# A fused attention, feed-forward and read/write layer on one core: the table of unit-matrix matmuls is emptied

## The reference

```python
x = x + layer(_layernorm(x), pos, ctx)     # read, attention, write, read, MLP, write
x = x + ffn(_layernorm(x))

def rat_read(res, W, gamma, beta, n):      # H = 256 channels of C = 4 copies
    y = einsum('blhc,hoc->bloh', res.reshape(b, l, H, C), W)
    return layernorm over h of y, times gamma plus beta

# attention: 16 heads of 16, rope, causal softmax over 512 rows, per batch
# rat_write: y @ wod.T, y @ wab.T + b, softplus and exp gates, hs * A + out * B

def _binary_diff_weight(w, base):          # for w1, w2, w3 (3584 x 1024 each)
    d = w - base
    return base + jnp.mean(jnp.abs(d)) * jnp.sign(d)
h = silu(x @ W1.T) * (x @ W3.T); out = h @ W2.T
```

## Time and profile before

| | before |
|---|---|
| time, median of 3 runs | 1188.22 us (1186.44, 1188.22, 1188.47) |
| the profiled execution | 1188.34 us |
| its span, first to last instruction | 1186.4 us |
| PE busy | 1156.8 us, 98% of the span |
| DVE, ACT, POOL busy | 913.4, 717.1, 473.5 us |
| mean granted clock of TensorE | 0.997 |
| unit-matrix matmuls (L1432) | 51, from 3.8 to 378.3 us |

### The profile page before, as it was taken

The page is one execution under the profiler, slowest core; times in us unless marked ns, Lnnn a source line. Parts: engine busy times, 40 slices in busy tenths (PEclk is TensorE's granted clock), DMA queues, the critical chain, the costliest instruction groups (busy, mean ns, idle before and its releaser), DMA issues.

```text
span 1186.4 us, 17254 instructions
## 1 busy us (share of the span) xinstructions
PE 1156.8 (98%) x6191; PEld 906.4 (76%) x6191; DVE 913.4 (77%) x1241; ACT 717.1 (60%) x1019; POOL 473.5 (40%) x593
## 2 busy tenths in 40 slices
PE   7998999999999999999999999999999999999998
PEld 5764666667777888877887888888888888888887
DVE  7766788688899778876797768777775777888764
ACT  5978679868776755665656656565663343333342
POOL 3778878886732543435333533355230000000000
PEclk9999999999999999999999999999999999999999
DMA  9677676673513686677866786668857978753242
GB/s 319 230 270 273 241 285 232 249 246 109 178 54 109 185 266 216 206 225 250 261 181 209 254 254 222 205 208 281 238 165 250 341 247 281 258 189 101 95 133 97
DMA packets 99160, 255.39 MB, mean 215 GB/s; under 512 B 9458, under 2 KB 24068, under 8 KB 98820
## 3 DMA queue, kind: packets, MB, share of 16 engines
q1 hardware_dynamic: 95044, 239.62, 57.5%
q0 software_dynamic: 4032, 14.68, 7.0%
HBM read 212.85 MB, written 41.42 MB: 214 GB/s over the span
## 4 chain that ended last, share of the span: by engine, by line
PE 50%; DMA 1%; issue 1%; DVE 1%; ACT 1%; POOL 1%; SPq 0%; ACTq 0%; DVEq 0%
PE pair L1590 19%; PE quad L1637 11%; PE pair L1637 11%; PE quad L1590 8%; DMA raw_base<-in_mean_w 1%; POOL raw_w L2592 1%; DVE ring_lo L2306 0%; DVE grid L2557 0%; ACT snap L2089 0%; DVE raw_w L2302 0%; ACT quad L1913 0%; ACT ring_hi L2073 0%; ACT ring_hi L1922 0%; ACT split L2125 0%; ACT hid L2128 0%
## 5 line engine op out<-in xcount | busy, mean ns | idle before, releaser
L2592 POOL TENSOR_TENSOR raw_w<-raw_w,raw_base 128x256 f32<-128x256 f32 x224 | 200.4, 941 | 178.5 <-DMA raw_base<-in_mean_w 178.5
L2125 ACT ACTIVATE split<-grid 128x1024 fp32r<-128x1024 f32 x98 | 104.0, 1061 | 160.8 <-PE pair L1637 147.7
L2534 DVE TENSOR_TENSOR split<-grid,split 128x1024 fp32r<-128x1024 f32 x98 | 119.7, 1225 | 61.8 <-ACT split L2125 61.6
L1637 PE MATMUL quad<-split 128*128 128x512 f32 x588 | 149.3, 389 | 0.5 <-DVE hid L2541 0.5
L1637 PE MATMUL pair<-split 128*128 128x512 f32 x588 | 149.2, 389 | 0.0
L1637 PEld LDWEIGHTS quad<-split 128*128 128x128 f32 x588 | 110.3, 188 | 23.7 <-DVE split L2534 0.9
L1637 PEld LDWEIGHTS pair<-split 128*128 128x128 f32 x588 | 110.4, 188 | 22.9
L2306 DVE TENSOR_TENSOR ring_lo<-raw_base,ring_hi 128x1024 fp32r<-128x1024 f32 x56 | 71.2, 1273 | 31.5 <-ACT ring_hi L2073 25.6
L1590 PE MATMUL pair<-t_b_hi,ring_hi 128*128 128x512 f32 x224 | 88.9, 397 | 2.1 <-ACT snap L2089 2.0
L1590 PE MATMUL pair<-t_b_lo,ring_hi 128*128 128x512 f32 x224 | 87.9, 392 | 0.0
L1590 PE MATMUL pair<-xnT_hi,ring_hi 128*128 128x512 f32 x224 | 87.5, 391 | 0.0
(11 more groups left out here) (328 smaller groups left out, 2779.0 us busy)
## 6 DMA issues: line engine op xcount, KB each, us to landing
raw_w<-in_w SPq DMA_DIRECT2D x56, 512.0 KB, 5.6
raw_base<-in_mean_w SPq DMA_DIRECT2D x56, 512.0 KB, 7.1
grid<-h_blocks SPq DMA_DIRECT2D x49, 512.0 KB, 4.0
late<-in_mean_w SPq DMA_DIRECT2D x28, 512.0 KB, 7.4
late<-in_w POOLq DMA_DIRECT2D x28, 512.0 KB, 7.1
grid<-in_mean_w SPq DMA_DIRECT2D x28, 512.0 KB, 4.9
h_blocks<-work SPq DMA_DIRECT2D x42, 256.0 KB, 2.7
ctxw<-in_w SPq DMA_DIRECT2D x20, 512.0 KB, 4.1
```

Of the source, the lines that this page charges most:

```text
L1637: a = pe.matmul(into[t], found[:, a, t * P:(t + 1) * P], found[:, b, :], start=p == 0 and n == 0 and q < 4, stop=p == PAIRS - 1 and n == 2 ...
L2125: act.activation(splits[n % RINGS][:, 0:2, :], operands(n), ACT.Copy).then_inc(a_hi, 1)
L2534: dve.tensor_tensor(found[:, 2:4, :], operands(n), found[:, 0:2, :].bitcast(F32), ALU.subtract).then_inc(a_lo, 1)
L2592: a = pool.tensor_tensor(w[:, some], w[:, some], base[:, some], ALU.subtract)
```

## The change

The table `LULLS` becomes empty. All 51 unit-matrix matmuls go, with the waits in front of them. Nothing else is edited: the order of all other steps, the banks and the buffers are the same. The whole diff, with rows of the table left out:

```diff
-LULLS = {
-    ('front', 0, 4): (14, 0, ('front', 0, 11)),
-    ('front', 0, 6): (4, 0, ('front', 0, 11)),
-    ('front', 1, 4): (10, 0, ('front', 0, 11)),
-    ('front', 0, 11): (1, 0, ('front', 0, 11)),
-    ('front', 1, 11): (1, 0, ('front', 1, 11)),
-    ('fill', 3, 0): (1, 0, ('fill', 3, 0)),
-    ('fill', 8, 0): (2, 6, ('weigh', 7, 0)),
...
-    ('turnmax', 13, 0): (2, 7, None),
-    ('finish', 6, 2): (2, 6, ('norm', 2, 1)),
-    ('finish', 6, 4): (1, 6, ('norm', 2, 1)),
-    ('turn', 3, 2): (1, 0, ('turn', 3, 2)),
-}
+LULLS = {}
```

## The result

The changed kernel takes 1190.43 us (median of 20 runs, 1187.27 to 1197.5), the kernel before, timed beside it, 1188.24 us (median of 20, 1184.43 to 1190.43). The ratio is 1.0024 with a 95% interval of 1.0013 to 1.0034: some 2.2 us slower by the medians (1.5 to 4.0 us by the interval), against the 1190.6 us that were forecast. Two executions of the unchanged kernel among the later runs, of 4842 and 2225 us, count in no ratio.

A forecast was written before the change was run, and what follows sets the result against it. PE, busy for 98% of the span, was taken to bound the kernel. 1188.34 us plus 2.5 for half clock at the start minus 0.2 for removed matmuls gave 1190.6 us; range for 8 in 10: 1188.3 to 1193.2 us.

The forecast's parts named there:

- The mechanism: Start of PE's timeline: without the first 14 matmuls PE is at half clock when tile 0 arrives; +2.5 us taken.
- The marks further on: Signs expected in the changed profile after the first product with `diag`, such as DVE's statistics of tile 1 at 24.6 to 25.3 us.
- Step 2: Tile 0's product with `diag`, 16 rows of 96 columns, at half clock: +0.8 us, bounds 0 and +1.8.
- Step 5: Gapless work from 19.45 us: full clock between 22 and 25 us; the product from 22.5 us costs 0 to 0.8 more.
- It cannot take back a delay of phase one: Feed-forward, from 360 us: runs as fast as PE does, so what phase one ends later, the kernel ends later.
- phase one carries the delay through: Tiles after the start: no slack in the ring of engines and late weight loads, so all of the 2.5 us stays.
- rival C: Between 50 and 180 us idle ACT and POOL absorb half or more of the 2.5 us: 1188.2 to 1189.4; chance 0.23.
- +2.5 - 0.2: Whole kernel: 2.5 us lost by half clock at the start, 0.2 us gained from the removed later matmuls.
- rival D: Attention: a third of the 21 later matmuls on the path, 1.5 us come back, faster at 1186.8 us; chance 0.08.
- The same two falls, at most one more: Later lulls: the clock falls twice as before, or once more, 1.65 us in the upper end of the range.

The follow-up runs named there:

- The run with the seam: Kernel before with 11 instead of 1 unit-matrix matmuls in the last group, at the begin of the feed-forward; 1188.57 us, ratio 0.9997.
- the rest alone: Kernel before without the first 28 unit-matrix matmuls (14 + 4 + 10), the 23 later ones kept; 1189.20 us, ratio 1.0001.
- 60 matmuls: Kernel before with 60 instead of 14 unit-matrix matmuls in the first group, ahead of tile 0; 1195.08 us, ratio 1.0052.
- the one with the lull filled: Kernel before with only the first 28 unit-matrix matmuls kept, plus 4 new ones in the lull near 306 us; 1187.73 us, ratio 0.9996.
- the kernel with transposes: Kernel before with the first group of 14 matmuls replaced by 28 fp32 transposes, all other groups kept; 1186.49 us, ratio 0.9972.
- the start alone: Kernel before with only the first 28 unit-matrix matmuls kept, the 23 later ones gone; 1186.13 us (0.9977), run again 1185.91 us (0.9981).

## Why the prediction was right in its sum and wrong in several terms

**The mechanism held.** "PE starts at half clock", and "the clock was raised by the first 14 matmuls": the kernels without them have the transposes of tile 0 at 1.94 us, those with them, or with transposes in their place, at 1.09 us or less. The first product with `diag` began at 13.40 us (forecast 13.6), and the rise came at 25.3 and 23.8 us (forecast 22 to 25). The marks further on were missed by about 1 us: the statistics of tile 1 began at 26.29 us (forecast 24.6 to 25.3).

**Step 2 was mis-sized.** I gave the product with `diag` +0.8 us, since its spacing was more than its columns need at full clock and "another limit, such as the weight loads, holds them". The argument took that limit as one that does not scale with the clock. It measured +1.73 us (3.73 against 2.00 us), next to the upper bound of +1.8: whatever holds these rows doubles too. From there DVE's statistics of tile 0 were 2.0 us late instead of 1.3, and the transposes of tile 1 began at 20.21 instead of 19.45 us.

**Step 5 was mis-sized.** For the second product I gave 0 to 0.8 us; it took 2.96 us against 2.0 in a profile in which the clock rose at 25.3 us, and 2.26 us where it rose at 23.8 us. The delay at this point was 3.8 us on DVE and 4.25 us at 43 us, where I had taken 2.5. The terms of steps 2 and 5 together make up 1.3 us of that 1.7 us; the last 0.5 us is the luck of the profile of before at 43 us.

**"It cannot take back a delay of phase one" did not hold.** I read it from the busy share of the feed-forward, 820.47 of 826.4 us. That leaves 5.9 us, of which 3.3 us lie behind the last matmul; the other 2.6 us are idle time between matmuls, and 2.0 us of them are waits for `snap`. That is as much as the whole effect in question. Of the 3.67 us at 361 us, 1.2 us were left in the span in one profile. In the other profile of the changed kernel all of its 4.5 us stayed. The run with the seam has it without any change in phase one: 2.2 us put in, nothing lost by the medians. And the rest alone came 3.8 us late to the feed-forward, where its interval of 0.9983 to 1.0018 allows at most 2.1 us. That the time comes back in the waits for `snap` fits the table, since the feed-forward is short where they are short; but they vary by more than the effect between executions of one program, and why they do was not tried. So the cause is argued, not shown. That phase one carries the delay through was right: 8.0 us became 8.6 us with 60 matmuls, and in the changed kernel nothing came back between 50 and 300 us, as rival C would have it (+4.3 and +5.0 us). Rival C had the right effect in the wrong place.

**The later matmuls were worth more than 0.2 us.** I counted "+2.5 - 0.2". With the start kept, taking away all of them gives 2.6 and 2.3 us, and taking away 20 of them 3.1 us (ratios 0.9977, 0.9981 and 0.9974); but a fourth kernel without them, the one with the lull filled, gives only 0.5 us (0.9996). The bounds were 0 and 4.6 us; rival D, with a third of them on the path, named 1.5 us. Told in this order, the errors cancel: emptying the start costs 4.3 to 4.9 us instead of 2.5, and 2.6 to 3.1 us come back instead of 0.2, which leaves 1.8 us in both sessions, beside the 2.5 - 0.2 = 2.3 us of the forecast. That the sum came out so near is luck. And the split depends on the order: with the later 23 kept, emptying the start costs 0.1 to 0.5 us, so the +2.5 us of the forecast is not a price that any pair of runs shows.

**Half-clock stretches.** "The same two falls, at most one more" was close: one and two in the two profiles of the changed kernel. But they follow the moment more than the table. The kernel before has its second one at 309.3 us in one profile and at 293.1 us in the other.

**What stays open.** Which of the later 23 cost the 2.4 us, and whether it is they: the unexplained 0.28% of the kernel with transposes and the missing gain of the one with the lull filled are of the same size. The single profiles do not show it: the start alone had spans 1.3 us above and 1.0 us below that of before, with the medians 2.3 to 2.6 us below. Nor is it settled why the later 23 help where the start is missing (1.0001 with them, 1.0024 and 1.0018 without; the intervals overlap), nor why the kernel with transposes at the start, which has all the later ones, is as fast as the best. The lull ahead of the row at 128.36 us was not tried.

## What to carry to other kernels

If PE's first work stands in a chain of short steps of several engines, keep it busy from the moment it can be, with anything, up to that work and through the first waits behind it: here 28 throwaway matmuls in idle time save 4 to 5 us of 1188 us by the medians if they are the only ones, though next to nothing if the later 23 are there too. Later ones of the same kind, placed one by one in lulls, must be measured: without them the time was 2.4 us lower in two runs of one kernel. And before you write that a stage cannot give back a delay, take what its busy share leaves (here 5.9 of 826 us), take off what lies behind its last instruction (3.3 us), and compare the rest with the effect in question. A single profile of each kernel does not settle effects of 2 us: the waits of one program differed by 4.7 us between two executions.

## What the runs showed of the hardware that was not expected

- At half clock even short float32 matmuls of 96 columns double: 16 of them took 3.73 us, against 2.00 us at full clock, although their spacing at full clock (0.11 us) is more than the 0.085 us that the rate of the 376-column rows would give.
- Transposes alone raised the clock: 28 of them, in float32, from 3.82 us on, and the next 8 took 1.09 us.
- The clock fell in the middle of work with small gaps (the longest wait 0.60 us), behind a stretch in which PE worked for 2.36 of 3.40 us, as well as after one wait of 3.07 or 3.50 us.
- When the clock rose, after the same work, differed between two profiles of the same kernel by 1.5 us (25.3 and 23.8 us).
